# The scores that serve the maximum on sixteen array tiles of 32 by 32 in place of four tiles of 32 by 128

## The reference

```
scores = einsum('bhqd,bhkd->bhqk', q, k) * scale      # layer 0: differential, 32 heads of 16
scores = where(causal, scores, finfo.min)             # layer 1: 16 heads of 32
probs  = softmax(scores); out = einsum('bhqk,bhkd->bhqd', probs, v)
```

## Time and profile before

| what | value |
|---|---|
| median of 3 runs | 2129.55 us |
| shortest and longest | 2128.58 and 2134.21 us |
| span of the profiled execution | 2127.3 us |
| busy: TensorE matmul, weight loads | 2057.7 us (97%), 1194.6 us (56%) |
| busy: VectorE, ScalarE, GpSimd | 1128.4, 518.8, 580.5 us |
| granted TensorE clock, mean | 0.992 |

### The profile page before, as it was taken

One profiled execution on the slowest core, in us unless ns is written; L12 is line 12 of the kernel. 1 busy time (PEld: TensorE's weight loads), 2 busy tenths in 40 slices (PEclk: granted clock), 3 DMA queues, 4 the chain that ended last, 5 costly groups with the idle time before them and its releaser, 6 DMA issues. The chain is left out here.

```text
span 2127.3 us, 32323 instructions
## 1 busy us (share of the span) xinstructions
PE 2057.7 (97%) x13439; PEld 1194.6 (56%) x13439; DVE 1128.4 (53%) x1731; ACT 518.8 (24%) x791; POOL 580.5 (27%) x548
## 2 busy tenths in 40 slices
PE   7899999999999999999999999999999999999996
PEld 5444444334444557556566655766666666666664
DVE  2567777567777744122222334364646464736567
ACT  2445555440000121101011122122222222222211
POOL 2222222128999600111110312022222222121122
PEclk9999999999999999999999999999999999999998
DMA  5101111205111147321211602100010101000000
GB/s 161 48 1 55 55 56 45 87 38 210 40 43 44 35 156 277 126 65 65 65 65 55 222 3 99 50 31 21 17 44 1 60 1 41 1 31 12 1 11 21
DMA packets 66237, 130.81 MB, mean 61 GB/s; under 512 B 6480, under 2 KB 19920, under 8 KB 66096
## 3 DMA queue, kind: packets, MB, share of 16 engines
q1 hardware_dynamic: 45968, 77.49, 11.1%
q10 hardware_dynamic: 14448, 32.64, 4.3%
q0 software_dynamic: 5680, 18.62, 3.0%
HBM read 97.40 MB, written 41.81 MB: 65 GB/s over the span
## 5 line engine op out<-in xcount | busy, mean ns | idle before, releaser
L1033 PE MATMUL conv_conv<-kv,toep 128*128 128x512 f32 x576 | 247.6, 592 | 0.3 <-POOL kv L1067 0.3
L2615 DVE RECIPROCAL tail_inv<-tail_ring 128x256 f32<-128x256 f32 x63 | 110.7, 1757 | 188.8 <-PE tail_ring L1935 188.3
L1623 PE MATMUL moe_gu_ps<-gu,xT_tile 128*128 x608 | 192.4, 459 | 0.0
L1033 PEld LDWEIGHTS conv_conv<-kv,toep 128*128 128x128 f32 x576 | 109.4, 190 | 139.0 <-issue 129.6
L1067 POOL TENSOR_TENSOR kv<-vT,cT 128x512 f32<-128x512 f32 x128 | 147.0, 1172 | 15.8 <-PE conv_conv L1033 12.0
L2302 POOL TENSOR_TENSOR tail_rstd_x<-tail_rstd_x,const_minus_half 128x2 f32<-128x2 f32 x31 | 21.8, 702 | 469.6 <-DVE tail_rstd_x L2577 469.6
L1623 PEld LDWEIGHTS moe_gu_ps<-gu,xT_tile 128*128 128x128 f32 x608 | 112.3, 190 | 66.5 <-issue 17.8
L2310 POOL TENSOR_SCALAR_AFFINE_SELECT tail_expT<-tail_expT 128x1024 f32<-128x1024 f32 x64 | 71.5, 1119 | 242.1 <-ACT tail_expT L2394 242.0
L2603 DVE TENSOR_REDUCE tail_negtop<-tail_scores 128x4 f32<-128x1024 f32 x64 | 78.2, 1221 | 95.6 <-PE tail_scores L1886 95.4
L594 POOL TENSOR_SCALAR_AFFINE_SELECT front_expT<-front_expT 128x2048 f32<-128x2048 f32 x32 | 64.3, 2008 | 199.1 <-ACT front_expT L649 199.1
L1604 POOL DMA_INDIRECT xg<-x_after,tokens x37 | 35.0, 947 | 282.3 <-PE moe_xT_ps L1618 255.2
(11 more groups left out here) (394 smaller groups left out, 3912.2 us busy)
## 6 DMA issues: line engine op xcount, KB each, us to landing
toep<-toeplitz SPq DMA_DIRECT2D x32, 320.0 KB, 2.9
y_slots<-moe_y ACTq DMA_DIRECT2D x39, 256.0 KB, 2.0
gu<-in_L_ffn_gate_up_proj SPq DMA_DIRECT2D x5, 1408.0 KB, 12.5
toeplitz<-filt_rows SPq DMA_DIRECT2D x8, 768.0 KB
front_e<-in_ctx SPq DMA_DIRECT2D x8, 512.0 KB, 4.7
toeplitz<-filt_rows SPq DMA_DIRECT2D x16, 256.0 KB
x_after<-x SPq DMA_DIRECT2D x8, 512.0 KB, 5.0
tail_x<-x_after SPq DMA_DIRECT2D x8, 512.0 KB, 3.7
```

The lines of the kernel that those rows point to most:

```text
L1033: ins = pe.matmul(bank, toep[p][:, mat * P:(mat + 1) * P], kv[p][:, c].rearrange("p b j i -> p (b j i)"), start=n == 0, stop=n == len(PART ...
L1623: ins = pe.matmul(gu_ps[:, s % 2, h, 0:HID], (xT if s else mid.xT_first)[:, c, :], wgu[c][:, e, h * HID:(h + 1) * HID], start=c == 0, stop ...
L2615: link.after(dve.reciprocal(inv[c % 2][:], bank[:, S:2 * S]))
```

## The change

Each score call of `score` is split by its queries into four calls of 32 queries, j outside and g inside, the order of the masks. So masks and scores run on the same sixteen tiles of 32 by 32. What is multiplied, the columns that each call streams, the banks and the semaphores stay as they are.

```diff
                         add_masks(pe, consts, lambda g, rows: bank[rows, g, :].rearrange("p (a k) -> p a k", a=2)[:, :, P:S], 2)
-                        for g in range(4):
-                            ins = pe.matmul(bank[:, g, :], q[strip(g), n, P:S], k[strip(g)].rearrange("p a k -> p (a k)"),
-                                            start=False, stop=True, skip_group_check=True)
+                        for j in range(4):
+                            for g in range(4):
+                                ins = pe.matmul(bank[strip(j), g, :], q[strip(g), n, P + 32 * j:P + 32 * j + 32],
+                                                k[strip(g)].rearrange("p a k -> p (a k)"), start=False, stop=True, skip_group_check=True)
                     else:
                         add_masks(pe, consts, lambda g, rows: bank[rows, g, :].rearrange("p (a k) -> p a k", a=4), 4)
                         for h in range(2):
-                            for g in range(4):
-                                ins = pe.matmul(bank[:, g, h * S:(h + 1) * S].rearrange("p (a k) -> p a k", a=2),
-                                                q[strip(g), 2 * (n - 4) + h, 0:P], k[strip(g), :, 0:P], start=False, stop=True,
-                                                skip_group_check=True)
+                            for j in range(4):
+                                for g in range(4):
+                                    ins = pe.matmul(bank[strip(j), g, h * S:(h + 1) * S].rearrange("p (a k) -> p a k", a=2),
+                                                    q[strip(g), 2 * (n - 4) + h, strip(j)], k[strip(g), :, 0:P], start=False, stop=True,
+                                                    skip_group_check=True)
...
-                    for g in range(4):
-                        s = slice(32 * g, 32 * g + 32)
-                        pe.matmul(bank[:, g, 0:S], q[s, P:S], k[s, 0:S], start=False, stop=False, skip_group_check=True)
-                    for g in range(4):
-                        s = slice(32 * g, 32 * g + 32)
-                        ins = pe.matmul(bank[:, g, S:S + P], q[s, 0:P], k[s, 0:P], start=False, stop=True, skip_group_check=True)
+                    for j in range(4):
+                        for g in range(4):
+                            s = slice(32 * g, 32 * g + 32)
+                            pe.matmul(bank[32 * j:32 * j + 32, g, 0:S], q[s, P + 32 * j:P + 32 * j + 32], k[s, 0:S], start=False, stop=False,
+                                      skip_group_check=True)
+                    for j in range(4):
+                        for g in range(4):
+                            s = slice(32 * g, 32 * g + 32)
+                            ins = pe.matmul(bank[32 * j:32 * j + 32, g, S:S + P], q[s, 32 * j:32 * j + 32], k[s, 0:P], start=False, stop=True,
+                                            skip_group_check=True)
```

## The result

The changed kernel takes 2149.34 us (median of 4 runs, 2144.43 to 2153.43), the kernel before 2129.07 in the same comparison. The ratio is 1.0092, 95% interval 1.007 to 1.0115: 20 us slower, where 17 us faster was forecast. The range, 2104 to 2131 us, does not hold it.

What follows compares the result with a forecast made beforehand. TensorE was taken to bound the kernel. 112 score blocks at 0.165 us saved gave 18.5 us, less 1.5 for waits and clock: 17 us off the median 2129.55, so 2112.5 us, range 2104 to 2131.

Steps and rivals of the forecast that it cites:

- TensorE is the bound, and what a block takes or gives goes to the end: Whole kernel: TensorE is busy 2057.7 of 2127.3 us, so shorter score blocks end it earlier by nearly the same amount.
- The gap between masks and scores is the change of tiling, 0.10 and 0.10 us: Score blocks before: switching from 32 by 32 to 32 by 128 costs 0.10 us emptying the array, 0.10 for an unhidden load.
- f32 on sixteen tiles runs at a tile's own rate: Score matmuls after the change: no pass gets longer or shorter, two passes of 256 columns taking 0.43 us.
- The stagger lies between 0.05 and 0.11 us: Score blocks after the change: the delay between the first tile and the last, bounded by 0.05 and 0.11 us.
- The sum without its stagger: Tail block after the change: load, mask columns, score passes and emptying; with stagger it was given as 0.93 to 0.98 us.
- Tiles take turns: Rival, score blocks: a tile's waiting second f32 pass holds up its strip's other calls; 2236 us, mild form 2142; chance 0.10.
- the instructions don't come fast enough: Rival, score blocks: supply too slow for 160 instructions, deciding from 6 ns each; 2160 us at 10 ns; chance 0.05.
- The floor of 25 ns between matmuls: Skill rule on matmul start-to-start time: each tail block would lose about 0.9 us; shares the slow-instruction rival's chance, 0.05.

Runs made afterwards that it cites:

- masks last: Kernel before, with front blocks of n under 4 on sixteen tiles, scores first and masks after them: 2129.09 us for 2128.77, ratio 1.0003.
- masks three times: Kernel before, with each mask added three times and scores on four tiles as before: 2168.62 us in one run.
- the two with bf16 stand-ins: Changed kernel, tail score calls given a bf16 constant for query and key: each call made twice 2131.49 us, each once 2101.47 us, one run each.

## Why the prediction was wrong

- *TensorE is the bound, and what a block takes or gives goes to the end.* Right: 23 us more in the blocks, 20 us in the median; 9 us less in them at the last, 9 in the median.
- *The gap between masks and scores is the change of tiling, 0.10 and 0.10 us.* Right. It is gone in the changed kernel, and with 32 by 64 throughout the block gains 0.10 us, though its masks take a round more.
- *f32 on sixteen tiles runs at a tile's own rate.* Right: without masks a second pass of 256 columns lasts 0.374 us on sixteen tiles and on four.
- *The stagger lies between 0.05 and 0.11 us.* This step failed. I took it from how fast instructions start when few are under way, and asked only for a limit on rate. What binds is how many are under way: with 160 in a block, the ninth tile waits for the first mask to complete, and the second set for passes of the first. In the first set the last tile starts some 0.30 us after the first (0.16 for the pause, 8 x 0.017 after it, 0.02 before it), and the second set adds about 0.2. The sum without its stagger is 0.88 us; with 0.30 and 0.2 it is the 1.38. (As they stand, the terms of the sum add up to 0.92 to 0.99 us and not 0.93 to 0.98, which is nothing beside that.)
- *The rivals.* "Tiles take turns" named the wrong mechanism. Nearest came "the instructions don't come fast enough", with its point of decision at 6 ns an instruction: a tail block has its 160 in about 1.2 us, 7.5 ns each. But they are not evenly spread, as that rival had them: they stop and go on. I gave it 0.05, because 32 instructions had gone at 1.7 ns. That row could not speak for more than 64. The most in any block of the kernel before is 64, and this should have widened the range: a count beyond what any row shows is an unknown cost, to be bounded from above by the length of the matmuls that could hold it up (0.28 and 0.37 us here).
- *The floor of 25 ns between matmuls* (the Trainium skill, "TensorE: Matmul & The Clock Gate", Part 1, as weighed in the prediction) does not fit f32 on different tiles either: in the kernel with masks last, sixteen second passes of 0.59 us span 0.69, 7 ns apart. The Trainium skill ("TensorE: Matmul & The Clock Gate", the table at its head) gives TensorE a queue of 64. The runs agree with the number and add that a place is kept until completion.

Whether the limit is 64 instructions, loads and matmuls together, or 32 matmuls the runs do not tell for certain, since every matmul here has its own load. The masks three times exclude that a pair of load and matmul keeps one place until both are done. Why instructions come at 4.2 ns after a wait and at 1.7 before it stays open too.

## What to carry to other kernels

When small matmuls are spread over more tiles, count the instructions under way together (f32 has two loads and two matmuls a call), not only the columns: once 64 are under way the next waits for a completion, and all behind it wait as well. A block may have more than 64 in all, as the 96 on tiles of 32 by 64, if the early ones complete in time. What paid here was one tiling for all parts of a block with fewer and larger tiles: 32 by 64 gave 9 us where 32 by 32 lost 20. Masks and scores both on 32 by 128 were not run. A burst in the trace shows a rate only for as many instructions as it has.

## What was not expected of the hardware

- 64 TensorE instructions between issue and completion: in six kernels (the changed one, masks three times, the two with bf16 stand-ins, no masks on sixteen tiles, masks last) a matmul beyond the 64th starts about 0.025 us after the recorded end of the instruction 64 before it (masks of 0.278 us: 0.30 to 0.32 after their start; of 0.385: 0.40 to 0.42).
- After such a wait instructions of the bf16 masks follow at 4.2 ns each, before it at 1.7.
- An f32 call's two passes do not hold up calls on other tiles of the same strip: of sixteen calls with 32 passes, all first ones start within 0.10 us.
